# A megakernel of two attentions and two mixtures of experts: preparation of the third and fourth part moved into the parts before them

## What is computed

```python
x = x + xattn0(layernorm(x), ctx)      # 16 heads of 64, softmax over 1601 keys
x = x + ffn0(layernorm(x))             # 8 experts 128->512->128 (gelu), gates from a
                                       # top-k over all (expert, token) scores, and a shared expert
x = x + xattn1(layernorm(x), ctx)
x = x + ffn1(layernorm(x))

def xattn1(x, y):
    Q = x @ Wq + bq;  K = y @ Wk + bk;  V = y @ Wv + bv
    K_hat = cos(K @ Wr + br)
    return softmax(Q @ K_hat.T) @ V

def ffn1(x):                           # 6 routed pairs of rank 16, the best 2 per token
    logits = x @ router_W.T + router_b
    w = top-2 of softmax(logits), made to sum to 1
    return x @ base_W.T + base_b + (x @ shared_A.T) @ shared_B.T \
         + sum_e w_e * ((x @ routed_A[e].T) @ routed_B[e].T)
```

## Time and profile before

| | us |
|---|---|
| median of 3 runs | 2023.85 |
| the runs | 2021.51 to 2027.93 |
| time of the profiled execution | 2021.12 |
| its span | 2019.4 |
| TensorE busy | 1871.3 (93%) |
| GpSimd busy | 1191.7 (59%) |
| VectorE busy | 1311.9 (65%) |
| ScalarE busy | 1126.1 (56%) |
| attention_0, about | 0 to 1505 |
| moe_0, about | 1505 to 1742 |
| attention_1, about | 1742 to 1976 |
| ffn_1 | 1976 to 2019 |

### The profile page before, as it was taken

How to read it: one execution, slowest core, us unless ns; L and a number is a source line. 1 busy time by engine, 2 the same in 40 slices (tenths; PEclk the granted TensorE clock), 3 DMA queues, 4 the chain that set the end, 5 groups by cost and what they waited for, 6 DMA issues and landing times. The chain is left out here.

```text
span 2019.4 us, 42416 instructions
## 1 busy us (share of the span) xinstructions
PE 1871.3 (93%) x16013; PEld 1453.7 (72%) x16013; DVE 1311.9 (65%) x3455; ACT 1126.1 (56%) x1616; POOL 1191.7 (59%) x670
## 2 busy tenths in 40 slices
PE   6999999999999999999999999999978899779995
PEld 4777777777777777777777777777755688557774
DVE  6576667666665766675666667666535777677755
ACT  4555555555555555555555555555457799544542
POOL 4666666666666666666666666676756354124450
PEclk9999999999999999999999999999988999879997
DMA  3000000000000000000000000000000221113200
GB/s 101 2 1 18 1 5 18 1 2 4 18 1 4 1 18 2 4 18 2 1 4 17 2 4 7 1 7 2 1 22 1 105 74 52 38 52 85 76 17 25
DMA packets 56412, 41.18 MB, mean 20 GB/s; under 512 B 2516, under 2 KB 53660, under 8 KB 55196
## 3 DMA queue, kind: packets, MB, share of 16 engines
q1 hardware_dynamic: 56220, 38.57, 6.4%
HBM read 37.45 MB, written 1.11 MB: 19 GB/s over the span
## 5 line engine op out<-in xcount | busy, mean ns | idle before, releaser
L544 POOL TENSOR_TENSOR a_den<-a_den,a_probs 128x1024 f32<-128x1024 f32 x352 | 838.3, 2382 | 383.6 <-ACT a_probs L794 382.6
L794 ACT ACTIVATE a_probs<-a_scores,a_mask_col 128x1024 f32<-128x1024 f32 x416 | 463.6, 1114 | 558.4 <-PE a_scores L674 509.7
L910 DVE CUSTOM_DVE_ANT_0 a_work<-a_work,a_mask_row 128x400 f32<-128x400 f32 (+1 forms) x1024 | 568.1, 600 | 214.4 <-PE a_work L584 211.2
L690 PE MATMUL a_pv<-a_probs,a_V 128*64 128x256 f32 x3328 | 405.1, 385 | 0.0
L690 PEld LDWEIGHTS a_pv<-a_probs,a_V 128*64 128x64 f32 x3328 | 220.3, 136 | 125.7 <-issue 24.5
L674 PE MATMUL a_scores<-a_shiftT,a_pick 64*128 64x256 f32 x1664 | 236.5, 276 | 0.0
L674 PEld LDWEIGHTS a_scores<-a_shiftT,a_pick 64*128 64x128 f32 x1664 | 161.1, 186 | 0.0
L910 DVE DVE_READ_ACCUMULATOR2_ANT a_maxes<- 128x1 f32 x1024 | 145.6, 142 | 0.0
L1106 DVE TENSOR_TENSOR m_h_lo<-m_h,m_h_hi 128x512 fp32r<-128x512 f32 x120 | 105.9, 895 | 50.8 <-ACT m_h_hi L1306 50.0
L670 PE MATMUL a_scores<-a_Q_hi,a_K_hi 64*128 64x256 f32 x832 | 127.1, 300 | 9.6 <-ACT a_probs L794 9.4
L773 ACT ACTIVATE a_V<-a_work 128x512 f32<-128x512 f32 (+1 forms) x224 | 124.7, 568 | 15.6 <-PE a_work L564 7.8
(11 more groups left out here) (354 smaller groups left out, 4104.8 us busy)
## 6 DMA issues: line engine op xcount, KB each, us to landing
m_gate_rows<-gate_scratch SPq DMA_DIRECT2D x8, 1024.0 KB, 4.8
a_c_nat<-in_ctx_dram SPq DMA_DIRECT2D x8, 768.0 KB
b_c_in<-in_ctx_dram SPq DMA_DIRECT2D x8, 768.0 KB
b_c_nat<-in_ctx_dram SPq DMA_DIRECT2D x8, 768.0 KB
m_w_raw<-in_L_ffn_W_dram SPq DMA_DIRECT2D x16, 256.0 KB, 4.8
a_acc<-in_x_dram SPq DMA_DIRECT2D x8, 128.0 KB, 2.1
out_dram<-tokens SPq DMA_DIRECT2D x4, 256.0 KB, 2.3
tokens<-in_x_dram SPq DMA_DIRECT2D x1, 896.0 KB, 9.7
```

Of the source, the lines that this page charges most:

```text
L544: nc.gpsimd.tensor_tensor(total, so_far, probs[:, buffer(c, j), :], ALU.add).then_inc(den_added, 1)
L690: last = nc.tensor.matmul(PV[HD * odd:HD * odd + HD, c % 2, queries], V[:, c % 2, j, h * HD:(h + 1) * HD], probs[:, buffer(c, j), first:fi ...
L794: nc.scalar.activation(probs[:, buffer(c, j), :].rearrange("p (o n) -> p o n", o=2), Sc[:, :, :], ACT.Exp, bias=mask_col[:, c // GROUPS % ...
L910: nc.vector.tensor_tensor_reduce(out=X[:, bank, :w], in0=X[:, bank, :w], in1=mask_row[:, off:off + w], scale=1.0, scalar=-3e38, op0=ALU.ad ...
```

## The change

Four things move. In **attention_0** the spread of an even stage goes behind the `k` items of its step instead of ahead of them. The loads of attention_1's weights, biases and first context are issued in **moe_0**, and in the steps of its last two experts ten items (`PREPARED`) make the transposed weights, `Wkr`, the first context's transposes and its angles, in the idle PSUM tensor `R`; both halves of a context's split are then VectorE's, and the last two instructions of each angle GpSimd's. In **attention_1** the queries are interleaved with the transposes, ScalarE makes the cosines ahead of the first copies of `xn`, and stage 0's scores stand ahead of the second context. In **the last stage of attention_1** twelve token tiles (`EARLY`) get statistics, root, scaling and transposes for ffn_1, whose loads SP issues behind its other ones; **ffn_1** does only the last four tiles, makes three of four logit products at once and eight of sixteen base products ahead of the spread weights.

```diff
@@ attention_0, raw_plan
         if s < STAGES:
-            middle[wides[5]].insert(0, (s, "spread", 0))
+            middle[wides[5]].insert(0 if c % 2 else len(middle[wides[5]]), (s, "spread", 0))
@@ moe_0
+    PREPARED = [("wT", 0), ("wkr", 0)] + [("cT", i) for i in range(4)] + [("angle", i) for i in range(4)]
+    PREPARE_AT = {(E - 1, 2 + 2 * n) if n < 7 else (E, 2 * (n - 7)): item for n, item in enumerate(PREPARED)}
...
@@ moe_0, SP, behind the loads of the first experts
+            for dst, src in next_loads:
+                sp.dma_start(dst, src).then_inc(CT.w_loaded, 16)
+            sp.wait_ge(consts, 1)
+            sp.dma_start(CT.c_in[:, 0:NC - 1, :],
+                         ctx_in[0, 0:(NC - 1) * P, :].rearrange("(c p) d -> p c d", p=P)).then_inc(CT.c_in_loaded, 16)
...
@@ moe_0, GpSimd
+                if c == E - 1 and it is None:
+                    query_weights()
                 if c >= 2:
                     for tg in range(TG):
+                        if c == E and tg > 0:
+                            finish_turns(tg - 1)
...
+            def finish_turns(i):
...
+                nc.gpsimd.tensor_tensor(t, t, n, ALU.subtract).then_inc(CT.angle_steps, 1)
+                pool.wait_ge(CT.angle_steps, 3 * i + 1)
+                nc.gpsimd.tensor_scalar(t, t, 0.5, -0.5, ALU.min, ALU.max).then_inc(CT.angle_steps, 2)
@@ moe_0, TensorE, at the end of a step
+                    if it is None and (c, k) in PREPARE_AT:
+                        prepare(*PREPARE_AT[c, k])
...
+                elif kind == "cT":
+                    pe.wait_ge(CT.c_in_loaded, 32)
+                    for ch in range(4 * i, min(4 * i + 4, NC)):
+                        last = nc.tensor.transpose(out[:, ch % 4 * P:(ch % 4 + 1) * P], CT.c_in[:, ch, :], ident[:, :])
@@ moe_0, VectorE, the same items
+                elif kind == "cT":
...
+                    nc.vector.tensor_copy(CT.cT[0][:, cols], out[:, :w]).then_inc(CT.c_hi_done, 1)
+                    dve.wait_ge(CT.c_hi_done, i + 1)
+                    nc.vector.tensor_tensor(CT.cT[1][:, cols], out[:, :w], f32(CT.cT[0][:, cols]), ALU.subtract)\
+                      .then_inc(prep_taken, 1)
@@ attention_1
-    PROLOGUE = numbered([(-2, kind, i) for kind in ("cT", "angle") for i in range(4)] +
-                        [(-1, kind, i) for kind in ("cos", "k_hi") for i in range(4)] +
-                        [(-1, "max", i) for i in range(8)] + [(-1, "shift", 0)] +
-                        [(-1, kind, i) for kind in ("cT", "angle") for i in range(4)], 0)
+    PROLOGUE = numbered([(-1, kind, i) for kind in ("cos", "k_hi") for i in range(4)] +
+                        [(-1, "max", i) for i in range(8)] + [(-1, "shift", 0)], 0)
+    NEXT_CONTEXT = numbered([(-1, kind, i) for kind in ("cT", "angle") for i in range(4)], 8)
...
+        if c == STAGES - 1:
+            for i, slot in enumerate((0, 0, 2, 2, 3, 3)):
+                slots[slot].append(("fstat", i))
+            slots[4].append(("faggr", 0))
+            slots[6].append(("frstd", 0))
+            for g in range(EARLY // 4):
+                slots[7 + g].append(("fscale", g))
+                slots[8 + g].append(("fT", g))
@@ attention_1, TensorE
+            transposes(0)
+            transposes(1)
+            queries(0)
+            transposes(2)
+            transposes(3)
+            for g in range(1, 4):
+                queries(g)
@@ attention_1, ScalarE
+            prologue("cos")
+            x_high(0)
+            x_high(1)
+            prologue("k_hi")
+            queries(0)
+            x_high(2)
+            x_high(3)
+            for g in range(1, 4):
+                queries(g)
+            exp(None, 0, 0)
+            for c, kind, i, use in NEXT_CONTEXT:
                 item(None, c, kind, i, use)
@@ ffn_1, TensorE
+            pe.wait_ge(small_done, 1)
+            for g in range(3):
+                nc.tensor.matmul(C[0:ROWS, g, :], smallT[:, :], xT[:, g * 512:(g + 1) * 512], start=True,
+                                 stop=True).then_inc(h_filled, 1)
...
+            pe.wait_ge(wb_done, 1)
+            for g in range(2):
+                base_products(g, A[:, g, :])
...
+            for g in range(2):
+                routed_products(g, A[:, g, :])
+                base_products(2 + g, C[:, g, :])
```

More of the change, by code:

```diff
@@ L1092, in experts @@
                 body(None, c)
-            with eng.Fori(0, E // 2 - 2) as it:
+            with eng.Fori(0, E // 2 - 3) as it:
                 for c in (4, 5):
                     body(it, c)
-            body(None, E)
+            for c in range(E - 2, E + 1):
+                body(None, c)
         def step_of(it, c, k):
@@ L1771, in item @@
                         last = nc.tensor.matmul(half, ones[0:1, :], bv_row[:, :], start=False, stop=True)
+                elif kind == "fT":
+                    pe.wait_ge(f_scaled, 4 * (i + 1))
+                    for t in range(4):
+                        last = nc.tensor.transpose(out[:, t * P:(t + 1) * P], FT.xn[:, 4 * i + t, :], ident[:, :])
                 last.then_inc(bank_full[bank], 1)
@@ L1893, in body, with x_high, queries, prologue @@
                             item(it, c, kind, i, use)
-            for c, kind, i, use in PROLOGUE:
+            def x_high(g):
+                act.wait_ge(xT_filled, g + 1)
+                nc.scalar.activation(xT[0][:, g * 512:(g + 1) * 512], Sc[:, g, :], ACT.Copy).then_inc(xT_hi_done, 1)
+            def queries(g):
+                act.wait_ge(q_filled, g + 1)
+                nc.scalar.activation(Qf[:, g * 512:(g + 1) * 512], PV[:, g % 2, :], ACT.Identity, bias=b_cols[:, 0:1])\
+                  .then_inc(q_done, 1)
+            def prologue(wanted):
+                for c, kind, i, use in PROLOGUE:
+                    if kind == wanted:
+                        item(None, c, kind, i, use)
+            prologue("cos")
[8 more added lines that the diff above has]
+            exp(None, 0, 0)
+            for c, kind, i, use in NEXT_CONTEXT:
                 item(None, c, kind, i, use)
-            exp(None, 0, 0)
             stages(act, body)
@@ L2003, in body @@
                         item(it, c, kind, i, use)
-            for c, kind, i, use in PROLOGUE:
+            for c, kind, i, use in PROLOGUE + NEXT_CONTEXT:
                 item(None, c, kind, i, use)
+            dve.wait_ge(q_done, 4)
             stages(dve, body)
@@ L2096, in _, with base_products, routed_products @@
         def _(pe):
-            pe.wait_ge(loaded, 128)
+            def base_products(g, bank):
+                for t in range(4):
+                    tok = slice((4 * g + t) * P, (4 * g + t + 1) * P)
+                    nc.tensor.matmul(bank[:, t * D:(t + 1) * D], xT[:, tok], Wb[:, :], start=(t == 0), stop=False,
+                                     skip_group_check=True)
+            def routed_products(g, bank):
+                pe.wait_ge(h_done, g + 1)
+                for t in range(4):
+                    tok = slice((4 * g + t) * P, (4 * g + t + 1) * P)
+                    last = nc.tensor.matmul(bank[:, t * D:(t + 1) * D], hT[:, tok], rbT[:, :], start=False,
+                                            stop=(t == 3), skip_group_check=True)
+                last.then_inc(y_filled, 1)
+            pe.wait_ge(FT.loaded, 128)
             pe.wait_ge(consts, 1)
@@ L2153, in _ @@
                                      bias=router_col[ER:ROWS, 0:1]).then_inc(logitsT_done, 1)
+            for g in range(3):
+                logits(g)
+            act.wait_ge(wb_filled, 1)
+            nc.scalar.activation(Wb[:, :], A[:, 2, 0:D], ACT.Copy).then_inc(wb_done, 1)
+            act.wait_ge(xT_filled, 1)
+            nc.scalar.activation(xT[:, 3 * 512:4 * 512], C[:, 3, :], ACT.Copy).then_inc(xT_done, 1)
+            logits(3)
             act.wait_ge(centred, 1)
```

347 lines of the change are left out of this document (212 added, 135 removed).

## The result

The changed kernel takes 1993.03 us (median of 4 runs, 1992.56 to 1994.03) beside 2023.64 us before: a ratio of 0.9847, 95% interval 0.983 to 0.9864. Forecast was 1997, with a range of 1989 to 2007. The profiled execution took 1994.03 us with a span of 1992.3; I had put 1994.1 and 1992.4. Between the two profiled executions lie 27.1 us, and the sum had 27.0. That the total is so close is partly luck: the terms are not. By the medians the change gave 30.6 us, 3.6 more than the sum, because the profiled execution before lies 2.5 us under its median and the one after 1.0 us above its own; where the other executions before lost their time no trace shows.

A forecast was written before the change was run, and what follows sets the result against it. TensorE was taken to bound the first attention and experts, a VectorE and ScalarE chain the two seams; -11.5 + 5.0 - 12.3 + 2.7 - 10.9 = -27.0 us gave about 1997 us on the median, range 1989 to 2007.

The forecast's parts named there:

- Spread: First attention: key products ahead of the spread's transposes hide TensorE's wait, 0.82 us in 14 even stages, 11.5 us less.
- a tie: First attention, even stages: ScalarE is free at 180.25, just when the next exponential, 0.9 us earlier, would be due.
- Lock moves to the odd stages: Rival, first attention: up to 15 odd stages wait 0.83 us for the nm write; +12.4 us, time 2009, chance 0.08.
- Experts: Last two experts: the added weight and first-context items cost TensorE 4.8 us; with 0.2 for a memset, 5.0 us more.
- The rival of stalls: Rival, experts: VectorE's lumps and GpSimd's extra work push h_lo past its slack ten times by 0.8; 2005, chance 0.12.
- Start of the second attention: First seam: earlier queries and maxima let TensorE resume at 1788.9 to 1789.2 instead of 1801.49, 12.3 us less.
- The rival of half the gain: Rival, first seam: the second context's angles stand alone before stage 0 while TensorE idles at half clock; 2003, chance 0.12.
- Last stage: Last stage of the second attention: early-tile transposes at 1.3 us and table loads at 1.4 us, 2.7 us more.
- The 1.4 us for table loads: Last stage of the second attention: two loads, 2.6 us in all, on the exponentials' path, about half covered by TensorE.
- The rival of the dearer table switch: Rival, last stage of the second attention: each table switch costs twice its load, 2.6 us; 2000, chance 0.05.
- Last part: Last part: only four tiles left makes the last logits' copy 9.3 us earlier, eight base products save 1.6; 10.9 less.
- Clock drop in the experts: Rival, last two experts: interruptions drop TensorE's granted clock to 1.2 GHz; +44 us, time 2041, chance 0.03.

The follow-up runs named there:

- experiment 1: The changed kernel run again with no edit: 1994.07 us, ratio 0.9854 to the kernel before.
- experiment 5: The changed kernel with GpSimd's third pair of angle instructions behind the last token add instead of ahead of it: 1991.47 us, ratio 0.984.
- experiment 2: The kernel before the change with the moved spread alone: 2013.41 us, ratio 0.9954.
- experiment 4: The changed kernel with the ten prepared items in ten steps in a row instead of every second step: 2001.44 us, ratio 0.9896.
- experiments 10 and 6: 6: changed kernel with the second context ahead of stage 0's scores, 1991.8 us; 10: that plus GpSimd's third angle pair behind the last token add, 1990.86 us.
- experiment 7: The changed kernel without the root of the twelve early variances and its two table loads in the last stage: 1994.63 us, ratio 0.9855.
- experiment 8: The changed kernel with stage 31's root in the first attention made on VectorE by bits and three Newton steps: 1997.56 us, ratio 0.9889.

## Why the prediction was right, step by step

- **Spread: mechanism and price right, the term 2.7 us too large.** 0.81 a stage were banked, where I had 0.82, and "a tie" on ScalarE was too cautious (0.46 us left). What stood in for the difference: 0.75 us in the first 133 us, and 1.6 us in the last stage, where the granted clock fell; by experiment 1 both are chance. The memset cost 0.14.
- **Lock moves to the odd stages: did not come.** Stage 17 alone waits, as before.
- **Experts: 4.8 forecast, 3.2 measured, a sum of misses.** The items cost what was forecast: against the kernel's own plain step of 1.36 us the ten add about 5.0 us to the last two experts, one of four transposes 0.49 (0.44 + 0.08 forecast). The step that failed is the one that priced GpSimd at nothing: the third pair, not only the fourth, stands ahead of the last add, 1.7 us on the path (experiment 5). The other way went a gain that the sum did not have: a plain step takes 1.36 us instead of 1.39. The four experts ahead of the last two take 88.1 to 88.4 us in every profile with the changed experts and 89.3 and 89.4 in the kernel before and in experiment 2, which has the old ones; with the last two that makes 2.0 us. TensorE's queue has a wait instruction of its own in each step before the change (32 in the 32 steps of two experts) and none there after it; that this is the reason no run tests. The last 1.4 us less lie in the first three experts, which take 94.7 to 96.6 us in profiles of the same code (97.0 before, 96.0 in experiment 2), so this is within chance. The rival of stalls was false at this spacing; at half of it one stall of 2.5 us came (experiment 4).
- **Start of the second attention: 12.3 forecast, 13.8 measured.** First maximum 6.8 us after the normalisation (7 forecast), shift at 12.3 (13.3), from there 19.6 to TensorE's resuming (19.8). The 3 us that I put on the scores ahead of the second context were real: 1.7 to 2.8 in experiments 10 and 6. The rival of half the gain did not come.
- **Last stage: 2.7 forecast, 3.5 measured, for another reason.** The 1.4 us for table loads are false (experiment 7). The transposes cost the 1.3 us forecast. In place of the loads stand TensorE's waits for VectorE's scaling, which I had at nothing: an idle of 0.6 us ahead of the second transposes, about 0.9 us with the gaps beside it. The closing products at the low clock add 1.2 us in this profile, 0.2 in experiment 1. The rival of the dearer table switch falls with them: with both switches gone nothing was gained.
- **Last part: 10.9 forecast, 11.3 measured.** Logit products took 1.5 us each, not 1.0, and the end gave 2.4 us, not 1.6. That the term fits is partly luck: over eleven profiles with the same last part it takes 31.4 to 33.8 us, at a granted clock of 0.80 in the shortest and 0.75 in the longest, so it is worth 9.7 to 12.1 us.
- **Clock drop in the experts: did not come**; the granted clock is 1.00 in the stretch.

## What to carry to other kernels

Work moved ahead of a wait on a full engine is banked only if what it delays is not the next thing waited for; look at both kinds of stage before the edit is made for all. When a serial chain on one engine sets a seam, put its inputs first and everything that another engine could do meanwhile behind them, even if that starts the main loop later. Of work added to an idle engine, ask what stands last in its queue at the end of the stage.

## What the runs showed of the hardware

- Some VectorE instructions that are issued while a large GpSimd add runs last until that add ends, however small they are. Of the 32 `nm` writes (128x8) of the kernel before, 15 met no add and took 0.17 us; 17 began while one ran, and each of them ended 0.03 us behind it, after 0.44 to 2.37 us. In experiment 8 four steps on 128x14 elements did the same (2.23 to 2.30 us, `TENSOR_SCALAR` and `SCALAR_TENSOR_TENSOR`). It is not so for every form: 20 reciprocals of 128x128 begun during such an add took 0.90 us on average, the others 0.92, and 61 `TENSOR_TENSOR` of 128x400 that read PSUM took 0.57 us, as the three outside an add did. The small `TENSOR_TENSOR` steps of experiment 8 never met an add, so they tell nothing.
- TensorE's granted clock can fall for some 4 us in the middle of a stage in one execution and not in the next of the same code, after gaps that stand in both (1.21, 0.97 and 1.21 us). Stretches of the same code differ between executions, with the lower clock in the longer one where the two are compared above: the start of the experts by up to 2.6 us, the last part by up to 2.4.
- A change of table cost nothing on the path where VectorE had work for the same time: two loads of 1.28 us, and experiment 7 gained nothing without them.
